# Two comparison operands of the aggregation loops are read from PSUM instead of SBUF

## What is computed

```python
h = relu(layernorm(x))
# first layer: two convolutions, each with a mean over the incoming edges
def sage_conv(x, src, dst, Wl, Wr, b):
    mean = segment_sum(x[src], dst) / max(count(dst), 1)
    return mean @ Wl.T + b + x @ Wr.T
x = x + sage_conv(relu(sage_conv(h, ...)), ...)
# second layer: a message for each edge, a mean over src
h = relu(layernorm(x))
msg = relu(concat(h[src], h[dst], edge_attr) @ W1 + b1) @ W2 + b2
x = x + segment_mean(msg, src)
```

## Time and profile before

| | us |
|---|---|
| median of 3 runs | 8933.78 (8912.83 to 8941.01) |
| span of the profiled execution, first to last instruction | 7514.0 |
| agg1, first to last indirect DMA of POOL | 146.26 to 2201.4 |
| agg2, the same | 2291.29 to 4381.9 |
| `place_edges`, the same | 4494.4 to 6509.7 |

### The profile page before, as it was taken

One profiled execution on the slowest core, in us unless ns is written; L12 is line 12 of the kernel. 1 busy time (PEld: TensorE's weight loads), 2 busy tenths in 40 slices (PEclk: granted clock), 3 DMA queues, 4 the chain that ended last, 5 costly groups with the idle time before them and its releaser, 6 DMA issues. The chain is left out here.

```text
span 7514.0 us, 144909 instructions
## 1 busy us (share of the span) xinstructions
PE 3521.3 (47%) x45080; PEld 3242.9 (43%) x45081; DVE 3895.5 (52%) x7026; ACT 1388.6 (18%) x2515; POOL 5335.9 (71%) x5308
## 2 busy tenths in 40 slices
PE   2222222222244333333333346666666666577778
PEld 2222222222233333333333336666666666566667
DVE  5555555555546556555555662121121211399997
ACT  2000000000000000000000022222222222388885
POOL 1777777777756777777777737777777777677774
PEclk8555555555555666656666665555555555699998
DMA  2111111111112111111111121111211111233332
GB/s 60 38 38 37 38 38 38 37 38 38 37 40 44 37 37 37 36 37 37 37 37 37 37 50 56 56 56 56 57 56 56 57 56 56 62 85 85 86 85 60
DMA packets 315377, 369.10 MB, mean 49 GB/s; under 512 B 177112, under 2 KB 177370, under 8 KB 315142
## 3 DMA queue, kind: packets, MB, share of 16 engines
q0 software_dynamic: 150528, 206.62, 12.0%
q1 hardware_dynamic: 163510, 161.65, 8.1%
q10 hardware_dynamic: 1298, 0.30, 0.0%
HBM read 298.33 MB, written 69.89 MB: 49 GB/s over the span
## 5 line engine op out<-in xcount | busy, mean ns | idle before, releaser
L599 PE MATMUL agg_sums<-agg_rows,agg_one_hot 128*128 128x64 bf16 (+1 forms) x18816 | 1080.0, 242 | 2788.2 <-DMA agg_rows<-h_table,agg_index 1525.4
L599 PEld LDWEIGHTS agg_sums<-agg_rows,agg_one_hot 128*128 128x128 bf16 x18816 | 1024.1, 131 | 2847.5 <-issue 2180.7
L572 POOL DMA_INDIRECT agg_rows<-g_table,agg_index x1568 | 1588.6, 1013 | 591.8 <-issue 482.1
L572 POOL DMA_INDIRECT agg_rows<-h_table,agg_index x1568 | 1554.1, 991 | 565.7 <-issue 500.4
L961 POOL DMA_INDIRECT sorted_edges<-place_rows,place_index x1568 | 1518.5, 968 | 584.0 <-issue 467.1
L1095 DVE COPY place_rows<-src_f 128x8 f32 (+1 forms) x196 | 34.8, 177 | 1526.9 <-DMA sorted_edges<-place_rows,place_index 1526.1
L578 ACT CAST agg_index<-src_f 128x8 uint32 (+1 forms) x392 | 77.1, 197 | 4053.5 <-DVEq L684 4045.6
L669 DVE TENSOR_TENSOR acc<-acc,agg_sums 128x130 f32 x392 | 114.1, 291 | 1326.8 <-PE agg_sums L599 1326.8
L1001 PE MATMUL place_rows_ps<-edge_attr_w,place_attr_t 128*128 128x64 f32 x3136 | 705.4, 419 | 0.4 <-PE place_rows_ps L979 0.4
L1001 PEld LDWEIGHTS place_rows_ps<-edge_attr_w,place_attr_t 128*128 128x128 f32 x3136 | 688.8, 331 | 0.5 <-issue 0.5
L991 PE MATMUL place_attr_ps<-ident,place_attr 128*128 128x128 f32 x784 | 212.0, 426 | 717.7 <-DVE place_hot L1060 703.8
(11 more groups left out here) (168 smaller groups left out, 5884.2 us busy)
## 6 DMA issues: line engine op xcount, KB each, us to landing
by_src_edges<-sorted_edges SPq DMA_DIRECT2D x293, 260.0 KB, 2.6
place_attr<-in_edge_attr SPq DMA_DIRECT2D x195, 256.0 KB
agg_rows<-h_table,agg_index POOLq DMA_INDIRECT x1568
agg_rows<-g_table,agg_index POOLq DMA_INDIRECT x1568
sorted_edges<-place_rows,place_index POOLq DMA_INDIRECT x1568
place_b_win<-b_table SPq DMA_DIRECT2D x196, 48.0 KB
h_table<-conv_in_rows SPq DMA_DIRECT2D x14, 336.0 KB, 2.7
g_table<-conv_in_rows SPq DMA_DIRECT2D x14, 336.0 KB, 2.7
```

Of the source, the lines that this page charges most:

```text
L572: pool.indirect_dma_start(rows[:, h, t, 0:PARTS * D], None, table, bass.IndirectOffsetOnAxis(ap=index[h][:, t:t + 1], axis=0)).then_inc(la ...
L599: mm = pe.matmul(to[:, 0:n], hot[:, t, :], rows[:, h, t, i * D:i * D + n], start=(i == 2 and t == 0), stop=(i == 1 and t == CH - 1), skip_ ...
```

## The change

In both classes the comparison in `members` reads its numbers 0 to 97 from the stage's PSUM copy `iota` and not from `k.iota` in SBUF. In `Ranking`, `places` is no tensor of its own in SBUF any more, but a part of the PSUM bank `before_ps` that is free by then, so that L831 writes it there and L832 reads it from there. The other input of each (`src_window`, `member`, `next_place`) stays in SBUF. Shapes, types, waits and the order of the instructions on every engine stay as they are; the PSUM tensor `iota` is allocated before the class is made, so that it can be handed over.

```diff
@@ sum_by_dst
-        s = sorting(k, o)
         iota = o.psum("iota", [P, 512])
+        s = sorting(k, o, iota)
@@ class Counting
-    def __init__(self, k, o):
+    def __init__(self, k, o, iota):
+        self.iota = iota
@@ members
-        link(dve, dve.tensor_tensor(self.member[:], wide(self.k.iota[:, 0:WINDOWS], 2, shape),
+        link(dve, dve.tensor_tensor(self.member[:], wide(self.iota[:, 0:WINDOWS], 2, shape),
                                     self.k.src_window[:, bass.ds(c, 1), :].to_broadcast(shape), ALU.is_equal), self.step, 5 * c + 4)
@@ class Ranking
-    def __init__(self, k, o):
+    def __init__(self, k, o, iota):
+        self.iota = iota
-        self.places, self.chosen, self.first = o.tmp("places", [P, WINDOWS]), o.tmp("chosen", [P, CH, WINDOWS]), o.tmp("first", [P, CH])
+        self.chosen, self.first = o.tmp("chosen", [P, CH, WINDOWS]), o.tmp("first", [P, CH])
         self.before_ps = o.psum("before_ps", [P, 4, P])
+        self.places = self.before_ps[:, 2, 0:WINDOWS]
@@ members
-        dve.tensor_tensor(self.member[h][:], wide(self.k.iota[:, 0:WINDOWS], 1, shape),
+        dve.tensor_tensor(self.member[h][:], wide(self.iota[:, 0:WINDOWS], 1, shape),
                           wide(self.k.src_window[:, bass.ds(c, 1), :].rearrange("p c t -> p (c t)"), 2, shape), ALU.is_equal).then_inc(self.members_ready, 1)
@@ sort
-        link(dve, dve.tensor_tensor(self.places[:], self.before_ps[:, 0, 0:WINDOWS], k.next_place[:], ALU.add), self.step, 5 * c + 1)
-        link(dve, dve.tensor_tensor(self.chosen[:], self.member[h][:], wide(self.places[:], 1, [P, CH, WINDOWS]), ALU.mult), self.step, 5 * c + 2)
+        link(dve, dve.tensor_tensor(self.places, self.before_ps[:, 0, 0:WINDOWS], k.next_place[:], ALU.add), self.step, 5 * c + 1)
+        link(dve, dve.tensor_tensor(self.chosen[:], self.member[h][:], wide(self.places, 1, [P, CH, WINDOWS]), ALU.mult), self.step, 5 * c + 2)
```

## The result

| | before | after |
|---|---|---|
| median of 4 runs | 8923.31 (8886.87 to 8941.01) | 9009.49 (8986.25 to 9021.2) |
| ratio | 1 | 1.0117 [1.0085, 1.0149] |
| span of the profiled execution | 7514.0 | 9005.1 |

The forecast was 8782 us, in 8735 to 8835. The span after is 1491 us longer than the one before, although the timed runs differ by 86. So the two profiles can't be subtracted. The span of before (7514) is that of an execution that went 1400 us quicker than the timed runs of the same kernel; the span of after is 4 us from its own time. Where such a difference lies is seen when the rows of after are held against the earlier trace rows.

What follows compares the result with a forecast made beforehand. The prediction took POOL's unbroken gather issues to bound agg1 and agg2; removing stalls of 54 us and 96 us, 150 in sum, should bring the timed 8933.8 us to about 8782, range 8735 to 8835.

Steps and rivals of the forecast that it cites:

- The stalls and their cause: Agg1 and agg2: gathers stall beside L741, L824, L832 because both inputs lie in SBUF; worth 54 and 96 us.
- DVE's price: L741, L824, L832 reading PSUM, and L831 writing it, cost nothing; upper bound 0.97 us more on each of the three.
- POOL issues without a pause: Agg1 and agg2: eight issues make a chunk of 10.0 us, so every stall removed shortens the stage.
- What is late next: Agg1 and agg2 without stalls: no other wait appears; small `Counting` operations cost 0, at most 25 us.
- DVE's wait at L669: Sign in both aggregations: DVE's wait for PE's sums, 4.1 and 2.7 us a chunk, shrinks after the change.
- Against the timed runs: Carries the 150 us gain from the 7514 us profile to the 8933.8 us timed median; 8782 us taken as likeliest.
- outside the stages: Variant: the 1419.8 us between profile and timed runs lies outside agg1 and agg2; gain 150, time 8784 us.
- everything slower by 1.189: Variant: whole program and its stalls are stretched by 1.189 in timed runs; gain 178, time 8755 us.
- a longer issue: Variant: only POOL's issues are longer in timed runs, 0.30 us on 1.26; gain 121, time 8813 us.
- no change: Rival: stalls have another cause or move, or POOL's issue doesn't bound the timed runs; 8934 us, chance 0.05.
- The rival "slower": DVE's PSUM reads or write so slow that DVE paces agg2; 9490 us at four times the length, chance 0.03.
- what would prove it wrong: Signs: long gathers remain beside the three operations, POOL pauses for indices, or the span falls by 150 without the timed runs.

Runs made afterwards that it cites:

- e8: Kernel before with only `places` moved to PSUM in agg2; prompt session, 7468.54 us, ratio 0.9918.
- e13: Kernel before plus a POOL memset of 1500 elements after each chunk's fifth gather, both aggregations; prompt session, 8132.88 us, ratio 1.0816.
- e14: Changed kernel plus a 1500-element POOL memset per chunk in both aggregations and `place_edges`; prompt session, 8459.03 us, ratio 1.1233.
- e17: Kernel before plus a 1500-element POOL memset after each chunk's fifth gather, both aggregations; late session, 8874.62 us, ratio 1.0087.
- e12: Changed kernel plus a 1500-element POOL memset after each chunk's fifth gather, both aggregations; late session, 8713.23 us, ratio 0.9806.
- e5: Kernel before with 16 instead of 48 matmuls a chunk in both aggregations; late session, 8812.37 us, ratio 0.9911.
- e6: Changed kernel with 16 instead of 48 matmuls a chunk in both aggregations; late session, 8757.36 us, ratio 0.985.
- e1: Kernel before, unchanged, timed and profiled again; late session, 8783.22 us, ratio 0.9991.
- e2: Kernel before with only agg1's edit (`Counting` comparison reads iota from PSUM); late session, 8794.04 us, ratio 1.0009.
- e3: Kernel before with only agg2's edits (`Ranking` comparison and `places` in PSUM); late session, 8855.58 us, ratio 1.0084.
- e10: Kernel before with four buffers for rows and indices instead of two, both aggregations; late session, 8878.02 us, ratio 0.9998.
- e11: Changed kernel with four buffers for rows and indices instead of two; late session, 8965.88 us, ratio 1.0086.
- e9: Agg2 changed in full, agg1 as before, plus a 640-element POOL memset after agg2's fourth gather per chunk; late session, 8897.61 us, ratio 1.0012.

## Why the prediction was wrong

Three numbers of each comparison say it: the change of POOL's busy time in a stage, that of the window, and the session.

| what went to PSUM | session | busy us | window us |
|---|---|---|---|
| e8, agg2 (first profile to e8) | prompt | -71 | -71 |
| with the long pause, agg2 (e13 to e14) | prompt | -44 | -37 |
| with the long pause, agg2 (e17 to e12) | late | -168 | -139 |
| with short matmuls, agg2 (e5 to e6) | late | -102 | -91 |
| agg1 (e1 to e2) | late | -26 | +2 |
| agg2 (e1 to e3) | late | -143 | +68 |
| four buffers, agg2 (e10 to e11) | late | -131 | +67 |

The rows of e8 and of e17 compare profiles of two sessions, the others of one.

By the prediction's own steps:

- **The stalls and their cause: right.** Gathers stand beside the three operations while both of their inputs lie in SBUF, and no more once one lies in PSUM. Busy 1499.76 and 1492.56 us for 1500 and 1493; longest 0.97 for "about 1.0". (By the starts and ends in the trace 721 gathers began inside an L640, not 747; none was long.) The Trainium skill, "SBUF — State Buffer", section "Who interferes with whom", infers that `tensor_tensor` leaves the interface free that descriptor generation needs. For this kernel's gathers the measurement decides against that inference: the longest in agg2 went from 1637 to 967 ns. The section's rule on operations with at most one input in SBUF, which leaves out the two-port modes, agrees with every gather beside the three changed operations. One gather in the first chunk of after took 1.72 us beside L732 and L733, which read one SBUF tensor each; whether they ran in such a mode no run shows.
- **DVE's price: right.** 963 to 971 ns from PSUM, the PSUM write of `places` 268 ns instead of 260, and the small operations of `Counting` cost nothing: POOL's busy time lies 7 us above 1568 x 0.952, 6.2 of them L1291's.
- **"POOL issues without a pause ... The time of both stages is the sum of POOL's issues", and under "What is late next": "PE and DVE keep 2 us of room, the indices come in time, and no other wait steps in": this step failed.** It was read from the one profile, and it holds in executions like that one. In the profiles near the timed runs TensorE came to its last matmuls late, its signal came up to 8 us after them, and POOL rested 885 us in agg1 and 774 in agg2 (e1) instead of 501 and 502. There the stall is not added to the chunk; it stands in the place of a part of that rest. Taking it out returned nothing in agg1 and cost 68 to 73 us in agg2. DVE's wait at L669, forecast to shrink, grew from 1327 us in the first profile to 1680 in that of after.
- **"Against the timed runs" named the gap and drew nothing from it.** All three variants (outside the stages, everything slower by 1.189, a longer issue) left POOL without a rest, so all gave a gain. In e1 the gap was 1262 us in the three stages, 1239 of them POOL's rest. Spread over 4704 gathers that rest is 0.26 us each, near the "0.30 us on 1.26" of the prediction. The sentence took it for a longer issue. The possibility that it was a wait had the chance of "no change", 0.05, although the profile was 16% shorter than the times to be predicted.
- **The rival "slower"** had DVE as the mechanism, which did not occur. The slower result came by a wait for the indices, which the prediction named only as what would prove it wrong.

Shown: the late matmuls and the late signal (the semaphore times, e6, e17), that fewer matmuls or more buffers don't take away POOL's wait for them (e5, e10), and that a pause of POOL shortens it (e9) or takes it away (e12, e17). That the stalls of agg2 worked as such pauses is argued. For it speaks that e9's pause gave TensorE back what the stalls had given it (4.2 and 4.3 us, against 7.7). But the stalls don't let the signals through themselves: in agg2 of e1 they fill 20% of the time, and 8 of the 163 signals over 0.5 us late came in one. And e5 to e6, where the change paid in a late session, shows that the price depends on something that these runs don't tell; no rule here gives its size. Open is why TensorE is late in some sessions, whether the whole changed kernel is faster in a prompt one (by the prediction's sum 150 of 7527 us; only half of agg2's change was measured there, -59 us), and whether a pause would help `place_edges` in a late one.

## What to carry to other kernels

Set the span of the profile beside the timed runs before anything else. When they differ by more than the effect that is to be predicted, the profile shows another regime, and its bound ("this engine never rests") must be given a large chance of not holding. A stall of the bounding engine is worth its length only if that engine doesn't wait elsewhere for something that comes late; ask of each microsecond taken out which later wait could grow. And time a kernel in more than one session: a part of this edit was 0.8% faster in the prompt kind, and the whole of it 0.7 to 1.2% slower in the late one; the same kernel was not run in both.

## What was not expected of the hardware

- One kernel took 7527 to 7531 us in some sessions and 8784 to 8888 in others, with the same instructions and the same durations of them (a gather's median 952 ns in both). In e1, 1239 of the 1262 us were POOL's rest in the three stages in which it issues gathers or scatters. What makes an execution late is open.
- In the late kind TensorE's instructions came singly at times, a pair of weight load and matmul every 1.41 us, and its semaphore increments up to 8 us after the matmul (24.6 us with four buffers, e10), while gathers were being issued. Of the increments over 3 us late in e1, 171 of 185 came while POOL issued nothing.
- TensorE's granted clock made no difference to agg1 in the kernels with 16 matmuls a chunk: 2328.54 us at 0.50 (1.2 GHz) in e5 and 2328.03 at 1.00 (2.4 GHz) in e6, which had 15 us of stalls less.
- A program that makes its bounding engine do 1.37 us of nothing in every chunk was, together with the change, 1.9% faster than before in a late session (e12). The same pause without the change was 0.9% slower in a late session (e17) and 8% slower in a prompt one (e13).
